# Attention over columns: x and the context also laid out model dimension first by the host, the first layer norm applied to columns with its moments spread through DRAM

## The reference, cut to what matters

```python
def _layernorm(x, axis=-1, eps=1e-05):
    m = jnp.mean(x, axis=axis, keepdims=True)
    v = jnp.var(x, axis=axis, keepdims=True)
    return (x - m) / jnp.sqrt(v + eps)
...
        qh = split_heads(q @ Wq)
        kh = split_heads(k @ Wk)
        vh = split_heads(v @ Wv)
        dots = jnp.einsum('bhid,bhjd->bhij', qh, kh) * SCALE
...
        attn = jax.nn.softmax(dots, axis=-1)
        out = jnp.einsum('bhij,bhjd->bhid', attn, vh)
...
    x = x + jnp.tanh(g_xattn[0]) * _L0_xattn_ref(_layernorm(x, axis=-1), ctx_1024, ctx_1024, ...)
    x = x + jnp.tanh(g_ffn[0]) * _L0_ffn_ref(_layernorm(x, axis=-1), ...)
```

## Time and profile before

| | us |
|---|---|
| median of 3 runs (lowest, highest) | 1763.51 (1763.26, 1765.22) |
| the profiled execution's own time | 1763.79 |
| its span, first to last instruction | 1761.5 |
| TensorE busy | 1690.0 (96%) |
| VectorE busy | 1332.0 (76%) |
| ScalarE busy | 1163.1 (66%) |
| GpSimd busy | 491.1 (28%) |
| mean granted clock of TensorE | 0.983 |

### The profile page before, as it was taken

The page is one execution under the profiler, slowest core; times in us unless marked ns, Lnnn a source line. Parts: engine busy times, 40 slices in busy tenths (PEclk is TensorE's granted clock), DMA queues, the critical chain, the costliest instruction groups (busy, mean ns, idle before and its releaser), DMA issues. The chain is left out here.

```text
span 1761.5 us, 36266 instructions
## 1 busy us (share of the span) xinstructions
PE 1690.0 (96%) x12148; PEld 1437.4 (82%) x12148; DVE 1332.0 (76%) x2255; ACT 1163.1 (66%) x3061; POOL 491.1 (28%) x365
## 2 busy tenths in 40 slices
PE   8999999999999999999999999989997999896998
PEld 6788888888888888888888888778885877775998
DVE  6767768677686676767767768876787999898885
ACT  5656666566666665666656666556765999796665
POOL 2322313323232232232322313320001766560000
PEclk9999999999999999999999999998998999897999
DMA  3210001100010010100110000015775886564664
GB/s 131 73 39 26 24 25 36 37 25 36 13 49 24 25 36 22 40 24 25 36 37 25 24 25 36 13 61 201 277 286 187 285 310 231 208 246 167 212 216 145
DMA packets 59998, 173.49 MB, mean 98 GB/s; under 512 B 4528, under 2 KB 34352, under 8 KB 57008
## 3 DMA queue, kind: packets, MB, share of 16 engines
q1 hardware_dynamic: 59952, 172.90, 28.2%
HBM read 96.86 MB, written 76.02 MB: 98 GB/s over the span
## 5 line engine op out<-in xcount | busy, mean ns | idle before, releaser
L377 POOL TENSOR_TENSOR prob<-prob,rsums 128x512 f32<-128x512 f32 x254 | 266.3, 1048 | 813.7 <-DVE rsums L571 667.2
L419 ACT ACTIVATE prob<-masked,neg_max 128x128 f32<-128x128 f32 x1024 | 396.3, 391 | 61.7 <-DVE neg_max L551 61.3
L419 ACT ACTIVATION_READ_ACCUMULATOR prob<-masked,neg_max 128x1 f32 x1024 | 194.3, 190 | 0.0
L567 DVE COPY probT<-trans 128x512 f32<-128x512 f32 x126 | 86.9, 690 | 130.4 <-PE trans L779 127.5
L551 DVE TENSOR_REDUCE neg_max<-masked 128x4 f32<-128x512 f32 x254 | 174.3, 686 | 8.8
L549 DVE TENSOR_TENSOR masked<-score,mask_add 128x512 f32<-128x512 f32 x254 | 172.8, 680 | 0.8
L779 PE MATMUL trans<-ident,prob 128*128 128x128 f32 x1024 | 160.6, 279 | 0.8 <-POOL prob L397 0.8
L428 ACT ACTIVATE probT<-trans 128x512 f32<-128x512 f32 x126 | 75.5, 599 | 119.0 <-PE trans L779 119.0
L434 ACT ACTIVATE qT<-proj 128x512 f32<-128x512 f32 x128 | 76.7, 599 | 111.1 <-PE proj L744 111.1
L804 PE MATMUL score<-kT,qT 64*128 64x128 f32 x2048 | 148.8, 285 | 0.0
L817 PE MATMUL y<-wo_hi,o_hi 128*128 128x256 f32 x508 | 145.9, 287 | 1.8 <-DVE wo_lo L499 1.8
(11 more groups left out here) (249 smaller groups left out, 4617.8 us busy)
## 6 DMA issues: line engine op xcount, KB each, us to landing
gate<-gate_d SPq DMA_DIRECT2D x30, 768.0 KB, 4.8
n_x<-n_x_d SPq DMA_DIRECT2D x25, 512.0 KB, 4.9
gate_d<-stage SPq DMA_DIRECT2D x8, 1536.0 KB, 6.1
n_u_d<-w_raw SPq DMA_DIRECT2D x16, 768.0 KB, 4.0
stage<-n_u_d SPq DMA_DIRECT2D x16, 768.0 KB, 6.0
gate_d<-gate SPq DMA_DIRECT2D x7, 1536.0 KB, 6.1
x_in<-in_x SPq DMA_DIRECT2D x16, 512.0 KB, 3.9
ctx_in<-in_ctx SPq DMA_DIRECT2D x16, 512.0 KB, 3.6
```

Source lines behind the costliest of these rows:

```text
L377: gp.tensor_tensor(pr, pr, rsums[:, h, :].rearrange("p (b o) -> p b o", o=1).broadcast_to([P, NB, P]), ALU.mult).then_inc(normed, 1)
L419: nc.scalar.activation(prob[:, c % 2, h, b, :], masked[:, h, b, :], ACT.Exp, bias=neg_max[:, h, b:b + 1], accum_out=psums[:, h, b:b + 1]). ...
L567: nc.vector.tensor_copy(probT[:, 1], trans[:]).then_inc(probT_copied[1], 1)
```

## The change

The host also gives `x_columns` and `ctx_columns`: x and the context with the model dimension first (256 rows of 8192 tokens). The context is now loaded in that layout and no longer transposed. x is still loaded by rows (for its statistics and the residual), and a second time by columns to `xt_in`. Except for the first group, which is still normalised by rows and transposed on TensorE, the layer norm is applied to the columns in place. A column layout needs mean and rstd along the free dimension, the same on every partition. So SyncE stores the two [128 x 4] tiles (now one tile `ln`) to DRAM in token order, 1024 elements of 4 bytes, waits for the store, and reads the 4 KB back to all 128 partitions (512 KB, `ln_rows`). GpSimd then subtracts the mean (`centre`, in its step 6), VectorE multiplies by rstd (`normalise`, first in its step 7), and both splits read SBUF in place of PSUM. The semaphores of the four later maxima (`amax_...`) are shared among the stages with counted values.

```diff
-        if c == NC - 1:
-            jobs += [(c, "t", n) for n in range(KC)]
...
             def load_ctx(g):
-                sp.dma_start(ctx_in[:], ctx[bass.ds(g * NB, NB)].rearrange("b p d -> p b d")).then_inc(ctx_loaded, 16)
+                sp.dma_start(ctx_in[:], ctx_t[:, bass.ds(g * T, T)].rearrange("(k p) t -> p k t", p=P)).then_inc(ctx_loaded, 16)
+
+            def load_xt(g):
+                sp.dma_start(xt_in[:], x_t[:, bass.ds(g * T, T)].rearrange("(k p) t -> p k t", p=P)).then_inc(xt_loaded, 16)
...
+            def spread_moments(g):
+
+                sp.wait_ge(rstd_ready, g + 1)
+                sp.dma_start(ln_d[:, g - 1].rearrange("o e b p -> p (o e) b"), ln[:], allow_slow_non_contiguous=True).then_inc(ln_stored, 16)
+                sp.wait_ge(ln_stored, 16 * g)
+                sp.wait_ge(xn_ready, g)
+                sp.dma_start(hand.xin[:, 0].rearrange("p b d -> p (b d)"),
+                             ln_d[:, g - 1].rearrange("o e b p -> o (e b p)").broadcast_to([P, 2 * T])).then_inc(ln_rows_loaded, 16)
+
             def load_next(g):
...
+                load_columns(g + 1)
+                if not (isinstance(g, int) and g == 0):
+                    store_x1(g - 1)
+                load_rows(g + 1)
+                spread_moments(g + 1)
+                if not (isinstance(g, int) and g == 0):
+                    store_xn2(g - 1)
...
+            def centre(g):
+
+                gp.wait_ge(xt_loaded, 16 * g)
+                gp.wait_ge(ln_rows_loaded, 16 * g)
+                gp.tensor_tensor(xt_in[:], xt_in[:], ln_rows[:, 0:1, :].broadcast_to([P, KC, T]), ALU.subtract).then_inc(x_centred, 1)
...
+            def x_high_part(g, k):
+
+                if k == 0:
+                    act.wait_ge(xn_ready, g + 1)
...
+                nc.scalar.activation(t_hi[0][:, k, :], xt_in[:, k, :], ACT.Copy).then_inc(x_high, 1)
...
+            def normalise(g):
+                dve.wait_ge(x_centred, g)
+                dve.wait_ge(ln_rows_loaded, 16 * g)
+                nc.vector.tensor_tensor(xt_in[:], xt_in[:], ln_rows[:, 1:2, :].broadcast_to([P, KC, T]), ALU.mult).then_inc(xn_ready, 1)
...
             def step(g, c):
                 u, new, soft, old, more = parts(g, c)
                 nxt = c == NC - 1 and new and more
+                if nxt:
+                    normalise(g + 1)
                 if soft:
...
-                if c == 6 and new and more:
-                    normalise(g + 1)
```

More of the change, by code:

```diff
@@ L98, in attention @@
             jobs += [(c, "v", NB + c - 2)]
-    jobs += [(NC - 1, "t", n) for n in range(KC, 2 * KC)]
     NJ = len(jobs)
[L101 to L107, removed]
+    FIRST = KC
+    assert NJ % 2 == 0 and FIRST == 2
     def jobs_of(c, kind):
@@ L129, in attention @@
         x_in = sb("x_in", [P, NB, D])
-        ctx_in = sb("ctx_in", [P, NB, D])
-        xn = sb("xn", [P, NB, D])
+        ctx_in = sb("ctx_in", [P, KC, T])
+        xt_in = sb("xt_in", [P, KC, T])
+        ln_rows = hand.xin[:, 0].rearrange("p b d -> p (b d)").rearrange("p (e t) -> p e t", e=2)
+        ln = sb("ln", [P, 2, NB])
+        mean, rstd = (ln[:, n, :] for n in range(2))
         xres = sb("xres", [P, NB, D])
@@ L387, in step @@
                     make_rstd(g + 1)
+                if c == 6 and new and more:
+                    centre(g + 1)
             make_rstd(0)
@@ L462, in _ @@
             w_high_part(1)
[L463 to L464 removed]
+            for k in range(KC):
+                x_high_first(k)
+            for k in range(KC):
+                ctx_high_part(0, k)
             w_high_part(2)
@@ L501, in _, with moments @@
             MOMENTS = NB + 6
-            def moments(stats, mean, var_eps, done, n, ready):
+            def moments(stats, mean, var_eps, done, n, ready, read=None):
                 v = nc.vector
@@ L511, in moments @@
                 dve.wait_ge(done, n + 3)
-                v.tensor_scalar(mean[:], m_sum[:], 0.5, None, ALU.mult).then_inc(done, 1)
+                if read is not None:
+                    wait(dve, *read)
+                v.tensor_scalar(mean, m_sum[:], 0.5, None, ALU.mult).then_inc(done, 1)
                 v.tensor_tensor(m_sq[:], m_dif[:], m_dif[:], ALU.mult).then_inc(done, 1)
@@ L677, in _ @@
             w_low_part(0)
-            normalise(0)
+            normalise_first()
             w_low_part(1)
-            for n in range(2 * KC):
-                low(-1, first_job(n), n, n)
+            for k in range(KC):
+                x_low_first(k)
+            for k in range(KC):
+                ctx_low_part(0, k)
             w_low_part(2)
@@ L737, in _, with product @@
             pe.wait_ge(consts, 1)
-            def product(b, before, stat, mov, n=KC):
+            def product(b, before, stat, mov, new_part=None):
                 wait(pe, copied[b], before)
-                passes = [(k, s, m) for k in range(n) for s, m in split(0, 1)]
+                passes = [(k, s, m) for k in range(KC) for s, m in split(0, 1)]
                 for j, (k, s, m) in enumerate(passes):
+                    if new_part is not None and (s, m) == (0, 0):
+                        new_part(k)
                     last = nc.tensor.matmul(proj[b][:], stat(s, k), mov(m, k), start=(j == 0), stop=(j == len(passes) - 1))
@@ L2019, in program @@
         w_raw = sb("w_raw", [P, 3 * IC * D])
+        peak = [st.enter_context(nc.semaphore(f"amax_{n}")) for n in ("local", "row", "top", "all")]
         before_n_p = ExitStack()
         hand = Handover(nc, before_n_p, G, D, KC, IC)
-        attention(nc, x, ctx, mask, g_xattn, wq, wk, wv, wo, bo, (w_up, w_gate, w_down), ident, ones, x1_d, xn2_d, w_raw, amax_x, wd, hand)
+        attention(nc, x, x_t, ctx_t, mask, g_xattn, wq, wk, wv, wo, bo, (w_up, w_gate, w_down), ident, ones, x1_d, xn2_d, w_raw, ln_d, amax_x, wd, hand)
         gate = sb("gate", [P, N])
@@ L2078 @@
     arrays, args = {}, []
+    inputs = dict(inputs)
+    for name, of in (("x_columns", "x"), ("ctx_columns", "ctx_1024")):
+        a = np.asarray(inputs[of])
+        inputs[name] = a.transpose(2, 0, 1).reshape(a.shape[2], -1)
     for name in INPUTS:
```

196 lines of the change are left out of this document (103 added, 93 removed).

## The result

The changed kernel takes 1954.8 us (median of 4 runs, 1952.7 to 1957.9), the kernel before 1763.5 on the same chip: a ratio of 1.108, 95% interval 1.107 to 1.110. The forecast was slower, at 1853 us, with a range up to 1895.

A forecast was written before the change was run, and what follows sets the result against it. TensorE was taken to bound attention, busy 99.55 of 100 us. `pv` 3.5 us later plus 2.5 us for the clock, at 15 boundaries, gave 90 us on top of 1763.79: 1853 us, range about 1815 to 1895.

The forecast's parts named there:

- The bound and the chain: Attention bound by TensorE; at group boundaries a serial chain from rstd through DRAM, GpSimd and VectorE delays `pv` by 3.5 us.
- The store, S = 4.1: Time for SyncE's store of the moments to land in DRAM: 4.1 us, between 2.6 and 5.6.
- The price for a piece: In the store of the moments, each additional piece costs 3.4 ns, so 1024 pieces take 5.6 us.
- Rival C: At the store, small pieces are dear: 11.1 us to land, 13.2 us lost a boundary, 1962 us; chance 0.12 (above 1895).
- Rival B: At boundaries, transfers quick, GpSimd sets the pace, clock kept: `pv` 1.4 us later, 1785 us; chance 0.21 with mixtures.
- The load, L = 3.9: Time for the moments to load back from DRAM to all partitions: 3.9 us, 3.5 at the least.
- The clock, 2.5 a boundary: Behind TensorE's idle stretch the granted clock drops to half speed, costing 2.5 us a boundary (bounds 0 and 2.75).
- That is 36.5 us, if nothing takes their place: Removing step 7's transposes and their wait saves 2.43 us at each of 15 boundaries.
- what costs nothing: Splits of context and x, GpSimd's subtraction beside softmax products, second load of x and moments' traffic: no cost.
- Rival D: At boundaries the chain hides and the transposes are saved, if multiplication is done by 438.79: 1727 us; chance 0.05.
- The same operations: Splits of context and x read SBUF in place of PSUM on ScalarE and VectorE, at no cost.

The follow-up runs named there:

- run 1: Changed kernel with the moments stored as 128 pieces of 32 bytes, so they return in the wrong order: 1823.3 us.
- run 2: Changed kernel with the 512 KB rows loaded early from columns of x, without waiting for the store of the moments: 1824.4 us.
- run 12: Changed kernel storing 1024 pieces of 4 bytes, each partition's 8 in 64 bytes of DRAM of its own, rows loaded from columns of x: 1879.7 us.
- run 13: Changed kernel storing 1024 pieces of 4 bytes, each in 64 bytes of DRAM of its own, rows loaded from columns of x: 1826.8 us.
- run 14: Changed kernel storing only the mean, 512 pieces of 4 bytes laid out as before, rows loaded from columns of x: 1935.0 us.
- run 15: Changed kernel with mean and rstd of a token side by side, stored as 512 pieces of 8 bytes, nothing left out: 1846.3 us.
- the fill: Changed kernel with 48 products of the identity with itself on TensorE ahead of its wait in a group's last step, results overwritten: 1937.8 us.
- run 3: Changed kernel without store, load, subtraction and multiplication for groups 1 to 15, whose columns are not normalised: 1754.6 us.
- run 6: Changed kernel, same result, with rows for statistics loaded separately and early, statistics and rstd in step 1, subtraction in step 5, multiplication in step 6: 1757.0 us, ratio 0.9964.
- run 8: The kernel of run 6 with the 32-byte tile `ln` allocated behind the large tiles: 1751.6 us, ratio 0.993.
- run 5: Kernel before, with only the context loaded by columns and not transposed; x still normalised by rows and transposed: 1762.5 us, ratio 1.000.
- run 10: Kernel before, with an unused 32-byte tile allocated ahead of `xres`, no instruction different: 1769.9 us, ratio 1.003.
- run 7: The kernel of run 6 with the second norm of the group before moved from VectorE's step 6 to step 5: 1779.8 us, ratio 1.010.

## Why the prediction was wrong, step by step

- **The bound and the chain: right.** The idle stretch, its place, the order of those who wait and the releasers are as forecast. rstd to store, the subtraction (2.34 for 2.39), the multiplication (1.23 for 1.22) and first mask to `pv` (435.75 - 431.12 = 4.63 for 4.70) were each within 0.1 us.
- **The store, S = 4.1: the step that failed.** "I take the middle of the first two, 4.1, since these pieces are small but many." It measured 8.7 to 11.5, mean 10.2. This alone is 15 x 6.1 = 92 us, near the whole miss of 102. The rows that I leaned on were stores and loads of pieces of 1 KB and more, whose number says nothing on pieces that lie close together in DRAM. The price for a piece also set the least of one row against the median of the other; least against least (2.6 and 3.5) gives 2.3 ns in place of 3.4. Runs 1 and 2 show what the store cost, 132 and 131 us without its pieces or without the wait for it, and runs 12 to 15 that it goes by how the pieces lie.
- **Rival C: nearly its time, another mechanism.** Its 11.1 came from 133 ns of an engine's time for each packet. In the group shown the packets were moved in 1.0 us; the 7.3 us behind that are a wait for completion. That the far end came close is luck, and the argument against it (the mean packet carries 2.9 KB) was beside the point.
- **Rival B: its order right, its clock wrong.** Run 1 has B's mechanism and loses the clock all the same, behind a gap of 4.1 us.
- **The load, L = 3.9: a little low.** From its issue to the subtraction it was 427.61 - 422.33 = 5.28 us in the group shown and 5.03 in the mean, 1.0 more than forecast with its hop, 15 us over the 15. Behind the quick stores of runs 1 and 13 the load lands in 3.6 us (medians; 4.6 in the changed kernel). The store of `xn2`, issued 0.5 us behind it at 14 boundaries, is not the whole reason, since the first boundary is without it and took 5.4; the cause stays open.
- **The clock, 2.5 a boundary: right, slightly high.** 0.88 us on `pv` and 1.2 in step 0 are 2.1 measured; the fill took 1.9 of it away (medians: step 7 from 21.24 to 20.38, step 0 from 11.18 to 10.17).
- **"That is 36.5 us, if nothing takes their place": too much.** Something does. With the whole chain out of the way (runs 3 and 6) step 7 falls from 9.75 to 8.75, not to 7.32: x's split is then last, which I had under "what costs nothing"; VectorE's wait of 0.30 us for it, which I struck out with the transposes, is still there (0.35 to 0.37 in runs 3 and 8). Rival D would have ended at 1752 to 1757 even so (runs 6 and 8). Its condition was also too mild: the multiplication done by 438.79 puts `pv` where it was, at 443.49. For 441.06 the masks would have to start at 436.36, while VectorE's second norm ends at 437.51. In the sum this was covered, since I walked the chain to `pv` itself.
- **"The same operations": not the same time.** Reading two SBUF tiles, the second low part of the context takes 1.45 us beside GpSimd (437.30 in the group shown of the changed kernel) in place of 0.69. There nothing waits for it; in run 5 TensorE does.
- **Not in the sum:** the 32 bytes that `ln` moves the large tiles by, some 5 to 8 us (runs 8 and 10).

By these terms: `pv` comes later by 314.8 / 15 - 9.75 - 0.88 = 10.35 us in the mean (3.5 forecast: S +6.1, L +1.0, the rest 0.3 the other way), 15 times 155 us; 15 x 2.1 = 31 for the clock, and some 5 for the other steps: 191, as the medians differ.

## What to carry to other kernels

When data crosses partitions by way of DRAM, look at how the pieces lie in DRAM, not only at their number and size: here the same 1024 pieces took 10.2 us packed together and 2.6 us spread out, and the time is not seen in the queue's busy share but between the store's issue and the next instruction that waits for it. A serial chain of store, load and two engines belongs several steps ahead of its use: moved there, with a store of 8.2 to 12.6 us, it kept no compute engine waiting. And before counting what a removed step frees, ask what is last without it: here 1.0 of 2.43 us came back. The best version, run 8, has the chain early and `ln` behind the large tiles, and still the packed store: 0.993 of the time before.

## What the runs showed of the hardware

- **Small pieces close together in DRAM** make a store's completion slow, long after its packets are moved (table above). The Trainium skill, "DMA: Bandwidth & Descriptors", section "Anatomy of one DMA", says of transfers that GpSimd issues that most of their fixed 2.0 us is the wait for the target memory's receipt; the prediction took that sum over for SyncE's. That the wait lies behind the packets agrees with the windows of the changed kernel, but from issue to the load behind it the same 4 KB took 1.44 to 11.5 us by layout, which a fixed time does not give. What the memory does meanwhile no run here shows.
- **VectorE waits for GpSimd** in some operations on SBUF: four `TENSOR_SCALAR` of 128x256 took 1.37 to 1.39 us alone and 3.09 to 3.50 beside a GpSimd subtraction of 2.39 (runs 1, 2 and 7), and a low part from two SBUF tiles 1.09 to 1.46 in place of 0.66 beside a softmax product that began ahead of it (the changed kernel and run 5), while masks and maxima on scores beside the same subtraction kept 0.68 and 0.69 (run 6). The trace of before had it in sight: the first norm took 2.08, beside a softmax product at 433.27, and the second, in the same operations, 1.39. The Trainium skill, "SBUF — State Buffer", section "Who interferes with whom", says that the two share a pair of ports under an exclusive lock, and that a tensor-scalar operation can claim it; the rows agree: in runs 1 and 7 the norm ends 1.1 us behind the subtraction's end, and each overlap costs 1.7 to 2.1 us.
- **A shift of 32 bytes** in the tiles that matmuls read made some products of 128x512 slower (389 to 396 ns for the line shown, none for x's low part), at a mean granted clock of 0.98 in all three runs, and the steps of attention but step 7 0.04 to 0.08 us longer (run 10).
